# Twenty matmuls of the identity ahead of TensorE's first product in a fused cross-attention and mixture-of-experts kernel

## What is computed

```python
# cross-attention, per sequence
n = layernorm(x)
q = (n @ Wq.T) * 16 ** -0.5 ; k = ctx @ Wk.T ; v = ctx @ Wv.T      # 16 heads of 16
x = x + (sigmoid(q @ k.T) @ v) @ Wo.T
# feed-forward, 16 experts of width 512, plus one shared unit
h = layernorm(x)
scores = softmax(h @ gate_w.T) ; w, idx = top_k(scores.T, 64)      # per expert
out = scatter_add(idx, (gelu(h[idx] @ Wg.T) * (h[idx] @ Wu.T)) @ Wd.T * w)
x = x + out + (gelu(h @ Ws_g.T) * (h @ Ws_u.T)) @ Ws_d.T
```

## Time and profile before

| | |
|---|---|
| time, three runs | 1361.31 to 1361.78 us, median 1361.59 us |
| span of the profiled execution | 1360.5 us |
| PE busy | 1325.6 us, 97% |
| ACT busy | 981.9 us, 72% |
| DVE busy | 632.1 us, 46% |
| POOL busy | 283.5 us, 21% |
| granted TensorE clock, mean | 0.996 |

### The profile page before, as it was taken

One profiled execution on the slowest core, in us unless ns is written; L12 is line 12 of the kernel. 1 busy time (PEld: TensorE's weight loads), 2 busy tenths in 40 slices (PEclk: granted clock), 3 DMA queues, 4 the chain that ended last, 5 costly groups with the idle time before them and its releaser, 6 DMA issues.

```text
span 1360.5 us, 22680 instructions
## 1 busy us (share of the span) xinstructions
PE 1325.6 (97%) x8882; PEld 760.0 (56%) x8882; DVE 632.1 (46%) x1260; ACT 981.9 (72%) x1144; POOL 283.5 (21%) x286
## 2 busy tenths in 40 slices
PE   5889999999999999999999999999999999999997
PEld 3434444444444444444444443324888888888887
DVE  4343245235325325423532631211657777777773
ACT  3558988888888898888888889998232445555553
POOL 1000011002002000200200200130000467766735
PEclk9999999999999999999999999999999999999999
DMA  6457774487379468558837936832533567878764
GB/s 172 126 129 166 120 156 133 117 136 204 110 125 187 135 114 169 144 117 130 213 104 130 184 117 81 150 132 79 185 125 124 171 179 177 209 188 192 192 119 47
DMA packets 119401, 196.85 MB, mean 145 GB/s; under 512 B 22752, under 2 KB 71904, under 8 KB 119296
## 3 DMA queue, kind: packets, MB, share of 16 engines
q1 hardware_dynamic: 99456, 161.44, 49.9%
q0 software_dynamic: 19648, 33.72, 12.6%
q10 hardware_dynamic: 192, 0.26, 0.1%
HBM read 118.99 MB, written 61.83 MB: 133 GB/s over the span
## 4 chain that ended last, share of the span: by engine, by line
PE 89%; ACT 5%; DVE 2%; issue 2%; DMA 1%; SPq 1%; POOL 0%; POOLq 0%; DVEq 0%; ACTq 0%
PE acc L1468 26%; PE score L1528 19%; PE score L1443 18%; PE score L1546 9%; PE misc L1350 6%; PE misc L1363 6%; ACT probs L757 5%; PE misc L1386 2%; PE misc L1371 2%; DMA keys<-key_parts 1%; SPq L480 1%; PE misc L1378 1%; DMA ctx_raw<-ctx_t 1%; PE score L1476 0%; PE misc L1401 0%
## 5 line engine op out<-in xcount | busy, mean ns | idle before, releaser
L757 ACT ACTIVATE probs<-score 128x1024 f32<-128x1024 f32 (+1 forms) x832 | 788.7, 1040 | 134.9 <-PE score L1443 128.7
L1468 PE MATMUL acc<-probs,values 128*32 128x512 f32 (+1 forms) x3328 | 413.7, 602 | 1.4 <-ACT probs L757 0.4
L1443 PE MATMUL score<-queries,keys 48*128 48x512 f32 (+1 forms) x1664 | 312.4, 449 | 8.6 <-DMA keys<-key_parts 5.6
L1443 PEld LDWEIGHTS score<-queries,keys 48*128 48x128 f32 (+1 forms) x1664 | 126.9, 180 | 265.8 <-ACT probs L757 200.1
L1468 PEld LDWEIGHTS acc<-probs,values 128*32 128x32 f32 (+1 forms) x3328 | 81.3, 109 | 182.5 <-issue 135.0
L630 POOL DMA_DIRECT2D ctx_raw<-ctx_t x32 | 23.4, 733 | 685.7 <-DVE ctx_lo L874 676.1
L767 ACT ACTIVATE gelu<-score 128x512 f32<-128x512 f32 (+1 forms) x100 | 57.4, 581 | 96.1 <-PE score L1528 95.5
L694 POOL DMA_INDIRECT gathered<-norm_scr,gather_row x64 | 81.3, 1270 | 203.6 <-DVE gather_row L1160 187.8
L1528 PE MATMUL score<-tok_hi,gu_hi 128*128 128x512 f32 (+1 forms) x400 | 120.7, 383 | 0.0
L1528 PE MATMUL score<-tok_lo,gu_hi 128*128 128x512 f32 (+1 forms) x400 | 120.0, 381 | 0.0
L1528 PE MATMUL score<-tok_hi,gu_lo 128*128 128x512 f32 (+1 forms) x400 | 120.0, 381 | 0.0
(11 more groups left out here) (187 smaller groups left out, 1438.5 us busy)
## 6 DMA issues: line engine op xcount, KB each, us to landing
keys<-key_scr SPq DMA_DIRECT2D x180, 200.2 KB, 9.2
key_scr<-key_parts SPq DMA_DIRECT2D x45, 512.0 KB, 5.1
gu_raw<-w_gu SPq DMA_DIRECT2D x17, 1024.0 KB
ctx_raw<-ctx_t POOLq DMA_DIRECT2D x24, 512.0 KB, 4.3
queries<-query_scr SPq DMA_DIRECT2D x180, 64.0 KB, 2.8
d_raw<-w_d SPq DMA_DIRECT2D x17, 512.0 KB
query_scr<-query_parts SPq DMA_DIRECT2D x15, 512.0 KB, 4.4
norm<-xn SPq DMA_DIRECT2D x224, 32.0 KB
```

The lines of the kernel that those rows point to most:

```text
L757: act.activation(probs[0:rows, n % RING, 2 * pair:2 * pair + 2, :], score[k % 3][0:rows, :, :], ACT.Sigmoid, scale=SCALE).then_inc(probs_d ...
L1443: mm = pe.matmul(score[k % 3][0:rows, g, :], keys[quarter % KEY_RING][of, pair, P * st:P * st + rows], queries[half][of, e, pair, :], star ...
L1468: mm = pe.matmul(acc[32 * c:32 * (c + 1), :], values[b % 2][0:rows, st, half, c, :], probs[0:rows, n % RING, c, :], start=(st == 0), stop= ...
```

## The change

PE waits for the identity at once, then multiplies it with itself twenty times (`EARLY`) into the first 128 columns of `misc`, and only then waits for the weights and the context. The wait for `const_ready`, which stood behind the first third of K, is moved ahead of these matmuls. Nothing reads what they write. `ident` is float32, so these are plain float32 matmuls, not transposes.

```diff
             first_k, first_q = first_bank[FIRST[2]], first_bank[FIRST[3]]
+            pe.wait_ge(const_ready, IDENTITY)
+            for _ in range(EARLY):
+                pe.matmul(misc[:, 0:P], ident[:], ident[:], start=True, stop=True)
             pe.wait_ge(w_first_hi, 1)
             pe.wait_ge(ctx_first_hi, 1)
             first_part(first_k, WK, (ctx_hi, ctx_lo), 0)
-            pe.wait_ge(const_ready, IDENTITY)
             pe.wait_ge(ln_first, 3)
             for task in FIRST[:2]:
                 product(task)
@@
 IDENTITY = 4
+
+EARLY = 20
```

## The result

The changed kernel takes 1355.18 us (median of 11 runs, 1354.36 to 1359.3), the kernel before on the same chip 1361.19 us (11 runs, 1355.7 to 1363.53). The ratio is 0.9965 with a 95% interval of 0.9954 to 0.9977: faster by 0.23 to 0.46%, 3.1 to 6.3 us. The forecast was 1359.2 us with a range down to 1357.2 us, and it called a change within 0.2% the likeliest. The span of the profiled execution is 1354.6 us against 1360.5 us, 5.9 us less. One run further down, of transp40, took 1452.6 us and is left out of that kernel's ratio.

What follows compares the result with a forecast made beforehand. PE carries 89% of the chain and is busy at full clock from 76.22 us, so only the start can gain: span 1360.5 - 2.4 = 1358.1 us, plus 1.1 us for the median, 1359.2 us; range 1357.2 to 1361.4 us.

Steps and rivals of the forecast that it cites:

- The early matmuls: PE from 3.0 us: 40 records priced like a float32 transpose, ending near 9.8 us under cover, cost 0 to 0.1 us.
- The lead at the query part: ACT's query part: at full clock Q ends sooner, so it starts at about 16.06 instead of 18.56 us, 2.5 us ahead.
- The lead at the key product and beyond: From the key product at 28.98 us to 72.7 us everything waits on each other, so the 2.4 us lead passes through.
- my bound of 2.5 us: At the first scores: lead between 1.6 us (SP's key DMAs) and 2.5 us (queries), taken as 2.4 us.
- the low stretch: Lower PE clock for 3.41 us at 28.44 us, covering one key product, worth 1.24 us; expected to stay, a little earlier.
- The sign that I had named: Forecast would be wrong if, among other things, a wait for SP's key DMAs stood ahead of the scores.
- The 3.95 us wait: PE idle before 72.81 us, with a 3.41 us low stretch behind: both stay, counted 0, up to 1.3 us either way.
- Carried to the end: From 76.22 us to 1356 us the change touches nothing, so whatever is won before is carried to the end.
- Rival 1: Around the scores: clock stays up, the key product is fast too, 3.6 us gained, 1358.0 us; chance 0.28.
- Rival 2: Before Q: clock falls again near 14.8 us, lead at the scores only 1.8 us, 1359.8 us; chance 0.22.
- Rival 3: At the start: early matmuls bring no clock rise, or idle time undoes it; 1361.6 us as before; chance 0.09.
- rival 4: Early matmuls: weight loads do not hide, the 40 records end at 18.6 us or later; 1365.7 us or more; chance 0.05.

Runs made afterwards that it cites:

- transp40: Changed kernel with forty transposes of the identity in place of the twenty plain matmuls; 1356.35 us against 1360.94 us, ratio 0.9967.
- a_again: The changed kernel unchanged, for a second trace and more times; 1356.47 us against 1360.62 us, ratio 0.9985.
- wait_only: Changed kernel with the moved wait but none of the twenty matmuls; 1359.97 us against 1360.62 us, ratio 1.0005.
- b_delay: Kernel before, with GpSimd's load of context chunk 1 of sequence 1 held until the second quarter's keys landed; 1356.82 us, ratio 0.9983.
- b_again: The kernel before unchanged, for a second trace; profiled span 1356.0 us.
- the held pair: Changed kernel and kernel before, both with GpSimd's load of context chunk 1 of sequence 1 held back; 1356.12 us and 1356.82 us.
- a_push: Changed kernel with one more DMA on SyncE's queue ahead of the last batch of twelve key DMAs; 1360.97 us against 1360.58 us, ratio 1.0013.
- a_look2: The changed kernel unchanged, for a third trace; profiled span 1356.3 us.
- a_fill: Changed kernel with thirteen more identity matmuls in TensorE's waits of 21 to 30 us; 1358.97 us against 1360.58 us, ratio 0.9997.
- early10: Changed kernel with ten early matmuls instead of twenty; 1357.0 us against 1360.94 us, ratio 0.9974.
- b_waits80: Kernel before with eighty more, long met waits on TensorE at its start, no early matmul; 1358.34 us against 1361.72 us, ratio 0.9985.
- b_swap: Kernel before with SyncE issuing the second quarter's first keys ahead of the queries; 1358.67 us against 1360.94 us, ratio 0.9992.

## Why the prediction was wrong, point by point

**The early matmuls: right.** Forty records, over at 9.42 us in the first trace and 10.6 us in a_again (forecast 9.8 us), start at 3.00 us. The nearest row for their price, the transpose, was the right one. In a_again they delayed the first product to 10.39 us and the transposes by 0.17 us, which is the 0 to 0.1 us of the text to within a tenth.

**The lead at the query part: right.** Forecast 2.5 us. From the start of the context rounding to that of the query part it takes 9.26 us in the trace of before and 6.73 us after, 2.5 us; against wait_only's 9.06 us it is 2.3 us. That it came out to a tenth is in part luck of the draw: in the nine traces without early work this way takes 8.04 to 9.26 us, the trace of before being the longest, and in the ten with twenty matmuls or forty transposes 6.71 to 6.86 us. In b_delay, the shortest of the nine, Q already ran at the full clock's pace. The lead is 1.2 to 2.5 us.

**The lead at the key product and beyond: the first step that failed.** I let 2.4 us "pass through", since everything waits on each other there. It held up to the first scores, where it was 3.4 us, above my bound of 2.5 us, and to the key product behind them. Then two things took it. SyncE's eighteen issues in a row lead by 1.6 us only (16.78 us before, 13.47 us after, less the chunk's 1.65 us), and I had ruled them out as a limit by looking at the scores alone; VectorE's split of the second key product needs the buffer that the last six of them empty, and waited for it until 28.84 us. And the low stretch, which I took to cost the same wherever it fell, moved from a key product onto the value product and the tasks behind it, or grew to 10.24 us in three of the traces with early work (in one without it, b_again, as well). At 43 us 0.4 us of the lead were left in the pair of first traces, minus 0.1 us against wait_only. Over all traces, counted from the rounding of the chunk, this key product comes 36.6 us later on average without early work (nine) and 35.8 us later with it and no filling (seven), a lead of 0.8 us. The size of this term was not 2.4 us; the held pair puts it at 0.7 us between medians. The sign that I had named, a wait for SyncE's key DMAs ahead of the scores, wasn't there: they held up VectorE and not TensorE.

**The 3.95 us wait: the second step, and the one that missed the time.** I wrote that the wait of 3.95 us at 72.7 us and the low stretch behind it stay, and gave them 1.3 us for the range. The wait was half chance: the trace of before showed an execution that had lost a race, which cost 2.45 us of landing and 1.6 us of clock. The rows for it stood in the trace (a context load issued at 68.05 us, the last key DMA at 68.49 us, a landing of 4.2 us against a median of 1.8 us), and I did not ask what the key DMA had to wait behind. This is worth 2.6 us between means, give or take 1.2 us, when it is removed alone (b_delay), and it comes back when it is put into the changed kernel (a_push, 4.5 us above a_again's median, on another chip).

**Carried to the end: only roughly.** I let a lead at 76 us pass on whole to the end. In the won traces, held ones among them, the way from the second quarter's scores to the end of the span takes 1285.9 to 1288.9 us, and in the three of the changed kernel 1286.3 to 1287.7 us, so up to 3 us come or go there that nothing here explains.

**The context chunk.** 1.65 us of the 5.9 us between the two first traces have nothing to do with the clock: the chunk was rounded at 9.30 us before and 7.65 us after. In the kernels without early work it came at 7.60 to 7.81 us in five traces and at 9.14 to 9.42 us in four; in those with twenty or forty at 7.62 to 7.66 us, once at 8.22 us, and with ten at 8.36 us. Whether the early work has a part in this is open. Nothing here shows how it could.

**The rivals.** Rival 1 (no low stretch around the scores) was right for the key product behind the scores, which ran at the full clock in the changed kernel's trace (24.85 us). But a low stretch followed at 30.47 us in that trace, at 26.18 us in a_again and at 37.25 us in a_look2; only in a_fill did the clock hold until 65 us. Rival 2 (the clock falls before the query product) happened in early10, not with twenty. Rival 3 and rival 4 fell: the clock rose in every trace with twenty, and the weight loads hid. None of the rivals was what happened, a change of timing on another engine's queue. The forecast had the direction right, but most of the gain came by a way that it did not have, and that is why the range was too narrow at its lower end.

What stays open: why the same kernel's packet comes at 57.6 us in one execution and at 61.4 us in another; and how the measured 0.35% (4.8 us) divides. From the runs, b_waits80 and b_delay put the race at 2.1 to 2.6 us of the 3.3 us between means of a_again and before, and the rest, about 1 us, is the early clock and perhaps the chunk's landing, each too small to be told from nothing.

## What to carry to other kernels

A single trace is one draw. Where a chain ends in a DMA that landed later than its like, look at what was issued within a microsecond of it, on every queue, before counting the wait as fixed. Work done early is kept only if every queue behind it can follow: read each one's slack (here SyncE's row of issues and the buffers that it frees), not only the one that ended last. And a change that only adds instructions can move instruction fetches and with them the order of DMAs elsewhere; a kernel with idle instructions in their place (here 80 waits; 20 had no effect on the time) helps to tell such a gain from the one that was meant.

## What the runs showed of the hardware that I had not expected

- A 16 KB packet of the instruction queue goes with one slow DMA issue on SyncE: 1.10 us at 61.64 us in the kernel before and 1.57 us at 48.00 us in the changed one, instead of 0.59 us. The last batch of twelve issues took 8.01 to 8.49 us in the eight traces with the packet inside it and 7.54 or 7.55 us in the twelve others. That the one causes the other is read from their standing together in the traces, not shown by taking one away.
- Transposes of float32 raise the clock: with forty transposes and nothing else on TensorE the later of them take 272 ns, the earlier ones 421 ns. The Trainium skill ("TensorE: Matmul & The Clock Gate", Part 4: PE-mode transpose) says that they don't count as busy work in the same way; this trace disagrees.
- The low stretches last 3.41 us or 10.24 us in the traces of one kernel (after and a_again), 6.83 us in others (b_swap, b_delay). With the longer one the tasks at 44 us came 1.4 us later.
- The time of the unchanged kernel spreads over 0.7% (1354.2 to 1363.9 us on one chip), and three runs within 0.5 us of each other, as stood ahead of the prediction, don't show that.
